# Attention in a three-attention network: transposes directly behind the next scores, three slots behind their own, with VectorE taking scores and maximum first

## The reference

```python
scores = einsum('bhqd,bhkd->bhqk', Q, K) / 4      # 256 x 77 for each of 16 heads
scores = scores + bias_or_mask                     # third attention: scores that are 0 become -1e30
attn = softmax(scores, axis=-1)
out = einsum('bhqk,bhkd->bhqd', attn, V)           # then merged heads @ Wo, added to x
```

## Time and profile before

| | us |
|---|---|
| median of 3 runs (1186.71 to 1192.58) | 1191.1 |
| profiled execution, device time | 1189.59 |
| its span | 1187.9 |
| PE busy | 915.3 (77%) |
| DVE busy | 567.6 (48%) |
| ACT busy | 424.1 (36%) |
| POOL busy | 404.0 (34%) |

### The profile page before, as it was taken

How to read it: one execution, slowest core, us unless ns; L and a number is a source line. 1 busy time by engine, 2 the same in 40 slices (tenths; PEclk the granted TensorE clock), 3 DMA queues, 4 the chain that set the end, 5 groups by cost and what they waited for, 6 DMA issues and landing times. The chain is left out here.

```text
span 1187.9 us, 18637 instructions
## 1 busy us (share of the span) xinstructions
PE 915.3 (77%) x5578; PEld 605.2 (51%) x5579; DVE 567.6 (48%) x1207; ACT 424.1 (36%) x820; POOL 404.0 (34%) x741
## 2 busy tenths in 40 slices
PE   6688757867229999963777867997999978877773
PEld 5455536643216777742444523664666655545541
DVE  4778845644431222225899713221121225777764
ACT  4355532312003333312666522221222213555644
POOL 5656634422470000016776411110000022666550
PEclk9899978968559999985899887998999996887885
DMA  5690001000121111124710030001111110000002
GB/s 169 241 327 1 1 4 45 0 10 0 49 102 49 62 62 62 62 68 159 293 32 19 1 107 22 23 26 58 36 44 44 40 46 14 15 14 14 1 1 71
DMA packets 60183, 71.25 MB, mean 60 GB/s; under 512 B 8172, under 2 KB 51924, under 8 KB 60116
## 3 DMA queue, kind: packets, MB, share of 16 engines
q1 hardware_dynamic: 55507, 57.81, 14.6%
q0 software_dynamic: 4608, 12.59, 3.2%
HBM read 45.73 MB, written 24.64 MB: 59 GB/s over the span
## 5 line engine op out<-in xcount | busy, mean ns | idle before, releaser
L1566 PE MATMUL PS<-WE,tmp 128*128 x496 | 185.8, 518 | 0.0
L1219 DVE TENSOR_TENSOR tmp<-PS,tmp 128x352 f32<-128x352 f32 (+1 forms) x78 | 47.4, 608 | 261.6 <-ACT tmp L858 261.6
L543 POOL TENSOR_TENSOR tmp<-tmp,small 128x616 f32<-128x616 f32 x96 | 116.7, 1216 | 102.1 <-DVE small L995 101.5
L1566 PEld LDWEIGHTS PS<-WE,tmp 128*128 128x128 f32 x496 | 91.5, 194 | 60.4 <-issue 36.1
L858 ACT ACTIVATE tmp<-PS 128x352 f32<-128x352 f32 (+1 forms) x78 | 41.4, 531 | 218.8 <-PE PS L1566 218.8
L771 ACT ACTIVATE tmp<-PS 128x768 f32<-128x768 f32 x96 | 77.9, 811 | 115.5 <-PE PS L1390 114.9
L1388 PE MATMUL PS<-ident,tmp 128*128 128x128 f32 x384 | 69.2, 309 | 45.1 <-POOL rsx L530 26.1
L1586 PE MATMUL PS<-WE,tmp 128*128 (+1 forms) x418 | 101.0, 380 | 2.1 <-DVE tmp L1231 2.1
L1301 PE MATMUL PS<-ident,XN 128*128 128x128 f32 x240 | 48.4, 337 | 68.2 <-ACT XN L707 54.0
L508 POOL DMA_INDIRECT WE<-ys,slot_u x32 | 32.5, 1015 | 182.4 <-DMA ys<-tmp 172.7
L644 POOL DMA_INDIRECT xs<-tmp,slot_u x48 | 46.6, 971 | 121.7 <-DVE tmp L1206 112.0
(11 more groups left out here) (210 smaller groups left out, 1620.8 us busy)
## 6 DMA issues: line engine op xcount, KB each, us to landing
tmp<-xs SPq DMA_DIRECT2D x62, 128.0 KB, 2.0
ys<-tmp SPq DMA_DIRECT2D x62, 128.0 KB, 1.7
xs<-WE SPq DMA_DIRECT2D x4, 1536.0 KB, 9.5
WE<-in_L_w SPq DMA_DIRECT2D x16, 352.0 KB, 6.9
WE<-in_L_rgT SPq DMA_DIRECT2D x8, 512.0 KB, 10.0
WE<-in_L_ruT SPq DMA_DIRECT2D x8, 512.0 KB, 10.2
WE<-in_L_rdT SPq DMA_DIRECT2D x8, 512.0 KB, 10.3
X<-in_x SPq DMA_DIRECT2D x8, 256.0 KB, 6.8
```

Of the source, the lines that this page charges most:

```text
L543: pool.tensor_tensor(sc, sc, spread(mx[:, q], SK), ALU.add).then_inc(shifted, 1)
L1219: dve.tensor_tensor(HH[:, q, 0:F], PS[:, 2 * q + 1, 0:F], SL[:, q, 0:F], ALU.mult).then_inc(hh_ready, 1)
L1566: last = pe.matmul(PS[:, 2 * q + k, 0:F], XS[:, q, c], w, start=c == 0, stop=c == G - 1)
```

## The change

The diff moves steps between slots and within them. Transposes go directly behind the scores of slot `s` and handle unit s-3 (they were last and handled s-2); values handle s-4 (they handled s-3). ACT's copy into `PT` moves up behind the exponential and handles s-3. DVE takes scores and maximum of `s` first, then the sums of s-2, then the residual. `OT` moves to odd slots. Output projection, residual, deviations and row transposes of the output side are one slot later (slots 0, 1, 2, 3), and the input side is two slots earlier (additions in slot 0, deviations in 1, transposes in 2; the gathers two slots earlier as well). Queries stay in slot 1. POOL's order within a slot is as it was. The buffers are as they were.

```diff
         def out_proj_slot(b):
-            return UNITS * b + 7
+            return UNITS * b + 8
         def residual_slot(b):
-            return UNITS * b + 8
+            return UNITS * b + 9
         def deviations_slot(b):
-            return UNITS * b + 9
+            return UNITS * b + 10
         def transpose_slot(b):
-            return UNITS * b + 10
+            return UNITS * b + 11
         def gather_slot(b, t, k, K):
-            return UNITS * b - 11 + t * 2 + k * (2 // K)
+            return UNITS * b - 13 + t * 2 + k * (2 // K)
         def add_slot(b):
+            return UNITS * b - 8
+        def in_deviations_slot(b):
+            return UNITS * b - 7
+        def in_transpose_slot(b):
             return UNITS * b - 6
-        def in_deviations_slot(b):
-            return UNITS * b - 5
-        def in_transpose_slot(b):
-            return UNITS * b - 4
...
                         act.activation(SC[:, k % 4], SC[:, k % 4], ACT.Exp, scale=FAR if stage == "a3" else 1.0).then_inc(exp_done, 1)
+                    if 3 <= s < NU + 3:
+                        u = s - 3
+                        act.wait_ge(pt_psum, u0 + u + 1)
+                        after(act, ot_ready, (u0 + u) // 2 - 1 if u >= 4 else 0)
+                        act.activation(PT[:, u % 4], PT_PSUM, ACT.Copy).then_inc(pt_ready, 1)
...
-                    if 2 <= s < NU + 2:
-                        u = s - 2
-                        act.wait_ge(pt_psum, u0 + u + 1)
-                        after(act, ot_ready, (u0 + u) // 2 - 1 if u >= 4 else 0)
-                        act.activation(PT[:, u % 4], PT_PSUM, ACT.Copy).then_inc(pt_ready, 1)
...
-                        if stage == "a3" and bi > 3:
-                            act.wait_ge(amax_taken, bi - 3)
+                        if stage == "a3" and bi > 4:
+                            act.wait_ge(amax_taken, bi - 4)
...
+                    if 0 <= s < NU:
+                        biased_scores(s)
+                    if 2 <= s < NU + 2:
+                        reciprocal_sums(s - 2)
                     b = batch_at(residual_slot, s)
                     if b is not None:
                         if stage != "a3":
                             dve.wait_ge(out_bias, B * layer + b + 1)
                         add_sum(stage, b)
-                    if 2 <= s < NU + 2:
-                        reciprocal_sums(s - 2)
-                    if 0 <= s < NU:
-                        biased_scores(s)
-                    if s % 2 == 0 and 4 <= s <= NU + 2:
-                        scaled_outputs((s - 4) // 2)
+                    if s % 2 == 1 and 5 <= s <= NU + 3:
+                        scaled_outputs((s - 5) // 2)
...
                     if 0 <= s < NU:
                         scores(s)
-                    if s == 3:
+                    if 3 <= s < NU + 3:
+                        transposes(s - 3)
+                    if s == 4:
                         pe.wait_ge(blocks_ready, 4 * (layer + 1))
-                    if 3 <= s < NU + 3:
-                        values(s - 3)
+                    if 4 <= s < NU + 4:
+                        values(s - 4)
...
-                    if 2 <= s < NU + 2:
-                        transposes(s - 2)
```

## The result

The changed kernel takes 1259.9 us (median of 4 runs, 1257.9 to 1261.3), the kernel before 1191.3 in the same session: 1.058 times as long, 95% interval 1.055 to 1.062. The prediction said 1231 us with a range of 1200 to 1258. The result lies 2 us above that range. The direction and the three waits were right, and the size was too small: +42 forecast, +68 measured between the profiled executions. The profiled execution after is 1257.89 us with a span of 1256.2, against 1189.59 and 1187.9.

The account below looks back on a forecast made before the run. PE and DVE both had little slack in a0, DVE bound a2's middle, nothing bound a3. Terms 13 + 2 + 6.7 + 15 + 5 = 42 on 1189.59 gave 1231 us, range 1200 to 1258.

Parts of the forecast that it names:

- the three waits: New stops walked through one a0 batch (Wait 1, Wait 2, Wait 3), making it 17.1 us against 14.50.
- Wait 1: a0 and a3, slot 1: queries wait for the residual to free bank 7; PE idles about 2 us, DVE 0.9.
- Wait 2: Slot 2: late reciprocals delay rsx, then deviations, normalisation and row transposes, holding the next scores; loss 1.5 us per a0 batch.
- Wait 3: Slot 0: POOL's late shift delays the exponential and ACT's copy, which PE's transposes need; loss 1.8 us per a0 batch.
- Five full batches of a0, +13: a0, slots 9 to 29: five batches, each 2.6 us longer, counted as +13 us.
- The run-up gives some 4 us back: Start of a0, before projection and residual are in it: some 4 us regained, with the last slots taking about as much.
- a2, +2: a2: part of Wait 2, 0.2 to 0.5 us a batch, plus one slot at the end; bounds -2 and +6.
- a3's start, +6.7: Start of a3: batch 1's row transposes now precede the value blocks in PE's order, delaying them 6.7 us with no cover.
- a3's batches, +2.5 each, 23.3 us: a3: each batch taken as 23.3 us, +2.5 for six batches, run-up and end cancelling, +15 us in all.
- Clock, +5: a0 and a3: more PE idle time lowers TensorE's granted clock, taken as +5 us, bounds 0 and +40.
- The prediction's own sign that the term is too small: Granted clock in a0 well under 0.9 in the profile after would show the clock term too small.
- the clock falls in every batch: Rival: projection and queries at 1.2 GHz in a0 and a3, +25 to +40 on top, about 1262 us; chance 13%.

Follow-up runs that it names:

- e9: Changed kernel plus unread extra TensorE matmuls in a0 and a3, behind scores of early slots and before values of each batch's slots 1 and 3: 1252.6 us, ratio 1.055.
- e2: Changed kernel with VectorE's old order (residual, sums, then scores and maximum), all else as changed: 1183.5 us, ratio 0.9955.
- e7: Changed kernel with batch 1's row transposes put back behind a3's value blocks and behind a2's slot 0 scores: 1254.3 us, ratio 1.056.
- e6: Changed kernel with VectorE's sums and reciprocals back in front of scores and maximum, residual still last: 1192.7 us, ratio 1.003.
- e8: Changed kernel with VectorE's order sums, residual, scores and maximum, and with the edit of e7: 1173.2 us, ratio 0.988.
- e1: Changed kernel plus four unread 128x128 matmuls behind the scores of stage slots 0, 2 and 3 in a0 and a3: 1257.1 us, ratio 1.059.

## Why the prediction was right in kind and too small

- **Nothing removed or added in work, only waits.** Right: the counts of a0 are the same in both windows.
- **Wait 1, 5.83 us from B1 to B2.** Measured 118.71 - 112.85 = 5.86, with 1.91 us in front of the queries.
- **Wait 2, B0 = B2 + 6.90.** Measured 108.57 - 101.56 = 7.01, with 1.18 us for the rows.
- **Wait 3, B1 = B0 + 4.34.** Measured 4.28. The copy is 0.33 us late. The batch of 17.07 in the walk is 17.15 in the trace.
- **Five full batches of a0, +13.** Measured +16.1. Three took 17.2 to 17.5 us. The two of 18.4 and 18.8 had a granted clock of 0.91, where the first two had 1.00. The end of the stage, set at about 4, took +4.4.
- **"The run-up gives some 4 us back": the first step that failed.** Up to B9 a0 lost 3.5 us, so this is 7.5 us off. I had thought of the missing projection and residual, and not of `rsx`, which is late in every slot from the first (1.24 us at 55.8), nor of a clock that stays at 0.50 while TensorE stands in pieces: 0.53 from 44 to 68 us, where the kernel before had 0.93. In e9, with 0.96 in that stretch, B0 to B5 is 4.0 us shorter.
- **a2, +2: the second.** It is +10.1. Its start has the same mechanism as a3's, which I did count: batch 1's rows in slot -2 are now in front of the first scores. VectorE at the start of a2, after:

```profile
577.55 0.80 DVE L991 TENSOR_TENSOR tmp<-PS,tmp 128x616 f32<-128x616 f32 x1 [5.05 <-PE PS L1379]
```

  and before:

```profile
548.38 0.77 DVE L991 TENSOR_TENSOR tmp<-PS,tmp 128x616 f32<-128x616 f32 x1
...
553.51 0.80 DVE L991 TENSOR_TENSOR tmp<-PS,tmp 128x616 f32<-128x616 f32 x1 [3.47 <-PE PS L1379]
```

  From the first gather to B0 that is 24.9 against 19.7 us, of which 2.2 come back by B9. In the middle, batches with additions take 18.2, 17.9 and 18.3 us against 16.7, not 0.2 to 0.5 more: twice a batch TensorE waits 1.57 us for `rsx`, which ScalarE makes here. As the additions now end a batch earlier, the fourth takes 15.1, and B9 to B29 is only 2.8 us longer. With VectorE's order undone (e2) such batches still take 17.0 to 17.6 us. There GpSimd's shift lies beside the additions, which take 2.8 to 3.4 us instead of 2.5, so the order is not all of it.
- **a3's start, +6.7.** Measured +6.3, by exactly the mechanism (ACT, then PE; compare):

```profile
1018.15 1.09 ACT L707 ACTIVATE XN<-X,SHIFTS,RSTDS 128x256 f32<-128x256 f32 x2 [3.69 <-POOL SHIFTS L488]
```

```profile
1019.38 1.09 PE L1301 MATMUL PS<-ident,XN 128*128 128x128 f32 x4 [5.56 <-ACT XN L707]
1020.26 1.91 PE L1344 MATMUL PS<-WE,firstrows 77*128 77x256 f32 x4
```

  But "with no cover" holds for the start alone: in e7 it came back at the blocks (7.4 us) and was lost again behind them.
- **a3's batches, +2.5 each, 23.3 us: the third.** Four of five took 24.0 to 24.2 us. In the third of them slots 1 to 2 took 8.1 (walked 7.9), 2 to 3 6.4 (6.4), 3 to 0 3.5 (3.5), 0 to 1 6.0 (what is left of 23.3: 5.5). VectorE, then TensorE's projection:

```profile
1135.12 0.80 DVE L987 SCALAR_TENSOR_TENSOR tmp<-PS,tmp 128x616 f32<-128x616 f32 x1 [3.10 <-PE PS L1390]
...
1141.53 0.80 DVE L987 SCALAR_TENSOR_TENSOR tmp<-PS,tmp 128x616 f32<-128x616 f32 x1 [3.75 <-ACT tmp L737]
```

```profile
1146.58 3.07 PE L1323 MATMUL PS<-W,tmp 128*128 128x256 f32 x8
```

  The first row names L1390, but L987 needs only the transposes of the unit four before, which are a slot old. ScalarE shows what it waited for, in the order that was walked (queries, normalisation, Z copy, which ends at 1134.99):

```profile
1132.84 0.60 ACT L727 ACTIVATE tmp<-PS 128x512 f32<-128x512 f32 x1 [4.62 <-PE PS L1331]
1133.33 1.08 ACT L707 ACTIVATE XN<-X,SHIFTS,RSTDS 128x256 f32<-128x256 f32 x2
1134.32 0.67 ACT L737 ACTIVATE tmp<-PS 128x616 f32<-128x616 f32 x1
```

  Two things failed. One is the base. Before, the batches were 21.04, 21.09, 20.86, 20.85 and 15.88 us: the last has no input side any more. After, they are 25.98, 24.22, 23.96, 24.02 and 23.98. So the last one loses 8.1 us where I had put 2.5, and the first loses 4.9. The other is that 24.0 is partly luck. It was walked for slow additions (2.57 us), but the last two batches have no additions and took 24.0 all the same: their slots 0 to 1 took 6.0 and 6.5 us, in batches whose clock is 0.79 and with projections of 2.9 us instead of 2.0. In e9, at 0.93 over these five batches, the same two steps take 4.5 us (walked by wait 3: 4.3), and the last two batches 21.9 and 21.0. Of the last batch's 8.1 us about 5 are therefore waits of the output side, and about 3 half clock.
- **Clock, +5.** The marks of e9 put at least 8 us on it, the ratios of the whole runs 4, so the sign and the order of size held. The prediction's own sign that the term is too small, a clock well under 0.9 in a0, came (0.87). The rival "the clock falls in every batch" gave 1262 us, nearest to the result, but by another way in a0: two of five batches fell, and at full clock they still take 17.15. In a3 it was partly true: all five batches lie between 0.74 and 0.86, and before they were at 0.86 together.
- **The Trainium skill, "TensorE: Matmul & The Clock Gate", section "What's actually happening"**, has throttled as the state that activity releases. The trace of a0 agrees (from 44 to 68 us 0.53 where TensorE idles in pieces, 0.96 with e9's fillers). a3's value blocks, below, do not: TensorE is busy without a gap for 13.60 us and stays at 0.50, and there the measurement decides.
- **What I had not seen:** that the three waits have one root. Wait 2 does name the late reciprocals, but I gave wait 1 to the residual's place and let waits 2 and 3 rest on GpSimd's order as well. e6 shows that the sums' place is enough: it takes back 67 of the 69 us by the medians. That the total comes out at the kernel before is partly a gain of the lag, since e2 and e8 are faster still. Wait 1 keeps half its length in e6.

What stays open: how the losses in the run-ups and in a3 divide exactly between clock and waits, because fillers cost time themselves; and why the clock falls in some of the equal a0 batches and not in others.

## What to carry to other kernels

When work is reordered on one engine, look at the smallest product that others wait for: 0.96 us of sums moved to the end of a slot cost more than everything else in the change, because GpSimd, ScalarE and TensorE are chained behind it in order. A walk through one steady batch predicts that batch well, but a stage also has a start, an end and batches with less work: put the new period against each of the old ones, not against the mean. And a change that loses may hold a part that gains: here the lag was good, and VectorE's order hid it.

## What the runs showed of the hardware

- TensorE can be busy without a gap and have half the clock: a3's value blocks, 77-row matmuls, 13.60 us busy of 13.60, with the granted clock at 0.50 (0.41 us for each of 33, as in the projections and queries at half clock, 3.30 us for 8):

```profile
1020.30:1033.90 13.60, 13.60 (x33) 10.75 (x33) 3.87 (x6) 0.60 (x1) 0.21 (x1) 0.50 0.04 14
```

- The additions of a2 (four instructions, 1.84 us alone) took 3.42 us in e8 when GpSimd's shift began 0.56 us after them (with a gather's issue on either side of the shift), and 2.51 before the change, when it had begun 0.33 us ahead of them. GpSimd's shift beside them kept its 1.22. In a3 of the change GpSimd paid as well: 1.38 us for a shift beside two additions of 1.90 together.
- The stages from the end of a0 to the first gather, which no edit touches, took 334.3 us in the kernels before and after and 330.1 in e1: 4 us between kernels for the same code. This is why the stages were compared by marks, and why differences of 2 to 7 us in the whole time (e1, e7, e9) say little by themselves.
